# Sheaf scans in two places of the next block, two output buffers in the message phase, no gathers for empty tiles

## The chip, the cores and the metric

The kernel runs on one core of a Trainium2 chip. The metric is the device time of one execution in microseconds (us); three executions were timed. Engines are called PE (TensorE), DVE (VectorE), ACT (ScalarE), POOL (GpSimd) and SP (SyncE, which only issues DMAs here).

## The reference

The kernel computes four graph layers over 3,125 nodes with 64 features and 100,000 edges sorted by destination, each followed by a layer norm of the sum with its input:

```python
edge_index = jnp.stack([src, dst])
x = _layernorm(x + _L0_gnn_ref(x, edge_index, edge_attr_32, ...))   # edge MLP, mean and max by destination
x = _layernorm(x + _L1_gnn_ref(x, edge_index, ...))                 # four attention convolutions
x = _layernorm(x + _L2_gnn_ref(x, edge_index, ...))                 # sheaf layer
x = _layernorm(x + _L3_gnn_ref(x, ..., src, dst))                   # attention by node
```

The two that are touched here work per edge. In L0 each edge gets h = MLP([x[row], x[col], edge_attr]) with three matrices, and h is summed and maximised by destination. In L2 two small MLPs per edge give two 4x4 orthogonal matrices, made from Householder parameters, and msg = Fve^T Fue x[row] is summed by destination:

```python
Fve = _householder(_mlp(cat_ve, ...))
Fue = _householder(_mlp(cat_ue, ...))
msg = jnp.einsum('eka,ekb,ebh->eah', Fve, Fue, xjr) * (dis[col] * dis[row])[:, None, None]
agg = jax.ops.segment_sum(msg.reshape(-1, D * H), col, num_segments=n)
```

## The kernel before, in words

The edges are padded to 102,400, that is 800 tiles of 128 edges in four quarters of 200 tiles (T, QT). Only 782 tiles (T2) hold edges; the last 18 of quarter 3 are empty. A block takes tiles from all four quarters at once, so that the partitions of a block hold four stretches of the sorted edge list, and a segmented scan along the free dimension gives running sums (or maxima) by destination.

**Message phase** (`message_phase`, 50 blocks of 4 x 4 tiles, lines 355 to 690). For each block DVE writes the source indices (`stage`, L512), POOL issues 16 indirect DMAs that gather rows of a table into `got_s` (L486), PE transposes them into the PSUM bank p1 on top of the product of the edge features (L631, L636), and the block then goes through a chain: DVE adds the destination part (L553), ACT applies the bias and relu (L672), PE multiplies (L643), ACT (L674), PE (L647), ACT (L676), DVE runs two scans (L557, L559), PE transposes their results (L651), ACT copies them into `out_t` (L679) and issues four stores (L684). Behind the stores ACT waits until they have landed (L685), before it takes the next block's `gate` (L670) and relu (L672). In the first 44 blocks DVE also makes one-hot matrices in bf16, eight instructions a block (L518), PE multiplies them (`counts`, L614, four calls a block) and DVE adds the products to prefix counts (`evict`, L535): these count edges for a later phase. Blocks 44 to 49 do without. DVE's order is written out by hand: `stage` of block b + 1 stands at the head of the body of block b, so behind the scans of block b - 1. POOL's gather for a block waits for its `stage` and for L636 of the block two before.

**Sheaf phase** (`sheaf_phase`, 25 blocks of 8 x 4 tiles, lines 1419 to 1816). Block 0 is a block of self loops that needs no gather; blocks 1 to 25 are the edges. POOL issues 32 indirect DMAs a block (L1553) into one of three buffers. ACT copies a part of the gathered rows (`sources`, L1769), PE makes the hidden layer and the Householder entries (`hidden_and_entries`, L1704 to L1716) with an ACT relu between (`hide`, L1764), and ACT writes the entries out (`entries_out`, L1779 to L1783). DVE then makes the matrices (`messages`: L1604 to L1621), computes q, gprod, g and the four terms (L1625 to L1642), and PE turns the terms into the scan's layout in four pieces (`to_scan` 0 to 3, L1728, 32 matmuls each). Two PSUM banks hold the pieces, so `to_scan` 2 and 3 need scans 0 and 1 to be done. DVE scans the four pieces of block n - 1 (L1663) in one place of block n, between L1621 and L1625, behind `along` (L1589, the destination part of block n + 1). PE turns the sums back (`sums_back`, L1740), ACT copies them (L1798) and issues four stores (L1802). PE's order in body n: `turn_rows` (L1695), `sums_back` of n - 1 with `to_scan` 2 and 3 inside, `hidden_and_entries` of n + 1, wait for the messages of n, `to_scan` 0 and 1. ACT's order: `roots` (L1773), the sums of n - 1 and their stores, `sources`, `hide` and `entries_out` of n + 1. `stage` (L1582) of block n + 2 stands at the head of DVE's body n. POOL starts the first gather when the phase's memsets are done (`ready`). SP loads the next block's rows and masks when the four scans are done (L1528).

The two lines around which the message phase's part of the change turns, and the loop of the sheaf scans:

```python
                        act.dma_start(quarter[q, b], out_t[:, :, q, :]).then_inc(out_st, 16)
                    act.wait_ge(out_st, b * 64 + 64)
```
```python
                for j, (k, h) in enumerate(PIECES):
                    dve.wait_ge(turned, n * 4 + j - 3)
                    dve.tensor_tensor_scan(run[k][h][:, :], cont2[k][r][:, 512 * h:512 * h + 512], pin[j % 2][:, :],
```

Of the kernel before, what the change touches and what calls it, by code (L numbers as in the profile page):

```python
# [354 lines left out]
def message_phase(nc, io, dram, keep):  # L355
# [5 lines left out]
    with phase(nc, "ms") as ph:  # L361
# [26 lines left out]
        out_t = ph.sb("out_t", [P, ST, 4, 2 * M])  # L388
# [5 lines left out]
        scanned, turned, masked, turned_out, out_st = (ph.sem(n) for n in ("scanned", "turned", "masked", "turned_out", "out_st"))  # L394
# [14 lines left out]
        prefix = dram["prefix"][ND5:, :].rearrange("(i d) (h l) -> (d h) i l", d=ND5, l=LOW)  # L409

# [61 lines left out]
        def _(pool):  # L472
# [3 lines left out]

            def body(it):
                for u in range(2):
# [117 lines left out]
        def _(pe):  # L596
# [25 lines left out]
            def body(it, counting, last):  # L622
                for u in range(2):
# [10 lines left out]
                    for i in range(ST):  # L634
                        pe.wait_ge(got[u][i], it * 64 + 64)
# [24 lines left out]
        def _(act):  # L660
            act.wait_ge(weights, 16 * 24)

            act.sem_inc(turned_out, 1)

            def body(it):
                for u in range(2):
# [16 lines left out]
                    for q in range(4):  # L683
                        act.dma_start(quarter[q, b], out_t[:, :, q, :]).then_inc(out_st, 16)  # L684
                    act.wait_ge(out_st, b * 64 + 64)  # L685

            with act.Fori(0, NB // 2) as it:
                body(it)
            for u in range(2):
# [729 lines left out]
def sheaf_phase(nc, io, dram, keep):  # L1419
# [6 lines left out]
    with phase(nc, "sh") as ph:  # L1426
# [64 lines left out]

        def is_block(n, *blocks):
# [47 lines left out]
        def _(pool):  # L1540
# [3 lines left out]
            def body(c, it):  # L1544
                u, r = c % 2, c % RING
                pool.reg_add(turn, turn, 1)
# [13 lines left out]
        def _(dve):  # L1560
            dve.memset(w2[:, :], 0.0).then_inc(zero, 1)
            dve.memset(got_s[0][:, :, :], 0.0)
            dve.memset(zin[:, :, :], 0.0)
# [15 lines left out]
            dve.sem_inc(messaged, RING - 1)  # L1579

            def stage(b, u):
                dve.tensor_copy(st_src[u][:, :, :].rearrange("p i k -> p k i"),  # L1582
                                keep["src"][:, :].rearrange("p (k t) -> p k t", k=4)[:, :, ds(b * SB, SB)]).then_inc(staged, 1)
# [9 lines left out]
            def messages(n, r, s, between=lambda: None):  # L1593
# [542 lines left out]
```

## Time and profile before

| | |
|---|---|
| median of three runs | 4694.56 us (4692.95 to 4698.24) |
| the profiled execution's own time | 4687.18 us |
| its span | 4685.4 us |
| busy share of the span | PE 63%, PE weight loads 47%, DVE 65%, ACT 27%, POOL 40% |
| message phase | 209 to 1413 us |
| sheaf phase | 3087 to 4277 us |
| granted PE clock, mean | 0.66 of full in 325 to 1290 us, 0.80 in 3497 to 4130 us |

The span is the time from the first to the last instruction of one profiled execution. A busy share says how long an engine worked, not whether the rest waited for it. Rows of a timeline give start, duration, engine, line, operation, output and inputs; in square brackets stands how long the engine had been idle and what ended the wait. PEld is PE's weight load. SPq, ACTq and the like are an engine's sequencer, here issuing DMAs.

### The profile page before, as it was taken

The page shows a single profiled execution, that of the slowest core. Times are in us where ns is not written, and L with a number is a line of the kernel's source. Part 1 is how long each engine was busy: PE and PEld are TensorE (multiplying, and loading weights), DVE is VectorE, ACT ScalarE, POOL GpSimd, SP SyncE. Part 2 cuts the span into 40 slices and gives each one's busy share as a digit, 9 for nine tenths or more (in the row PEclk, how much of TensorE's full clock was granted, in tenths as well). Part 3 has the DMA queues.
Part 4 walks back from the last instruction along what each step waited for, and adds up shares of the span by engine and source line. Part 5 has one row for each costly group of instructions (what it writes and reads, how often), then busy time and mean ns, then how long its engine had stood idle before and what let it go on. Part 6 is the DMA issues. An engine that isn't in the chain of part 4 may idle for free. (4 is left out here: it accounts for less than half of the span.)

```text
span 4685.4 us, 59450 instructions
## 1 busy us (share of the span) xinstructions
PE 2968.8 (63%) x19382; PEld 2193.7 (47%) x19382; DVE 3034.2 (65%) x4651; ACT 1274.4 (27%) x1892; POOL 1881.9 (40%) x1835
## 2 busy tenths in 40 slices
PE   1055556566642477779799699515766667673676
PEld 1034444344421254546556466315665666663455
DVE  9466676667623488756556466446677767774796
ACT  0011111111110277535345245101111111110484
POOL 4577777677762121100000000067777677642000
PEclk9966666666665699989899899657878788876698
DMA  5156666555630488534234144044454554541342
GB/s 178 33 136 152 155 154 150 145 149 149 153 83 13 184 333 325 202 132 157 77 144 160 60 152 149 1 91 86 100 120 100 106 118 93 114 85 26 111 167 73
DMA packets 738112, 599.57 MB, mean 128 GB/s; under 512 B 486055, under 2 KB 676612, under 8 KB 714476
## 3 DMA queue, kind: packets, MB, share of 16 engines
q1 hardware_dynamic: 462650, 389.91, 28.4%
q0 software_dynamic: 64032, 141.68, 10.5%
q10 hardware_dynamic: 211282, 66.03, 6.0%
q8 instruction: 91, 1.49, 0.1%
q14 instruction: 57, 0.47, 0.0%
HBM read 396.80 MB, written 200.61 MB: 128 GB/s over the span
## 5 line engine op out<-in xcount | busy, mean ns | idle before, releaser
L486 POOL DMA_INDIRECT ms_got_s<-table_src,ms_st_src x800 | 845.7, 1057 | 339.8 <-issue 332.1
L1553 POOL DMA_INDIRECT sh_got_s<-sheaf_src,sh_st_src x800 | 783.9, 980 | 301.9 <-issue 239.2
L1728 PE MATMUL sh_pin<-ident,sh_term 128*128 128x128 f32 x3200 | 465.5, 317 | 129.0 <-DVE sh_run L1663 114.5
L1728 PEld LDWEIGHTS sh_pin<-ident,sh_term 128*128 128x128 f32 x3200 | 455.8, 232 | 135.1 <-DVE sh_run L1663 120.2
L1047 DVE CUSTOM_DVE_ANT_0 c_xs<-c_pa,c_logs 128x1024 f32<-128x1024 f32 (+1 forms) x400 | 379.0, 967 | 187.9 <-PE c_pa L1154 109.5
L126 POOL DMA_INDIRECT spread<-dst_tab,first_idx x25 | 24.3, 971 | 1133.1 <-DVEq L100 1125.8
L991 PE MATMUL c_pa<-c_esT,c_v 128*64 128x128 f32 (+1 forms) x5000 | 399.8, 286 | 86.2 <-DVE c_esT L1061 61.7
L991 PEld LDWEIGHTS c_pa<-c_esT,c_v 128*64 128x64 f32 (+1 forms) x5000 | 278.0, 138 | 224.7 <-issue 119.3
L973 PE MATMUL c_pa<-ident,c_xs 128*128 128x128 f32 x2500 | 370.3, 287 | 0.0
L1154 PE MATMUL c_pa<-c_kT,c_q_st 64*128 64x512 f32 (+1 forms) x800 | 340.7, 546 | 43.4 <-DVE c_peaks L1047 27.7
L614 PEld LDWEIGHTS ms_pc<-ms_hot_l,ms_hot_x 128*125 128x125 bf16 x1408 | 211.5, 208 | 283.6 <-issue 263.5
L614 PE MATMUL ms_pc<-ms_hot_l,ms_hot_x 128*125 128x256 bf16 (+1 forms) x1408 | 240.0, 342 | 148.5 <-DVE ms_hot_l L518 148.5
L1017 ACT ACTIVATE c_xs<-c_xs,c_neg 128x1536 f32<-128x1536 f32 x200 | 317.8, 1589 | 56.5 <-DVE c_neg L1056 56.1
L1157 PE MATMUL c_pa<-c_kT,c_q_st 64*128 64x512 f32 x600 | 323.0, 647 | 0.0
L535 DVE TENSOR_TENSOR ms_sums<-ms_pc,ms_sums 125x256 f32<-125x256 f32 x704 | 297.3, 422 | 27.7 <-DVE ms_run_max L559 9.6
L973 PEld LDWEIGHTS c_pa<-ident,c_xs 128*128 128x128 f32 x2500 | 276.9, 143 | 70.9 <-issue 70.6
L1011 ACT ACTIVATE c_esT<-c_pa 128x512 f32<-128x512 f32 (+1 forms) x400 | 203.8, 514 | 368.9 <-PE c_pa L973 368.3
L1061 DVE COPY c_esT<-c_pa 128x512 f32<-128x512 f32 x300 | 206.6, 689 | 137.0 <-PE c_pa L973 136.6
L1663 DVE TENSOR_TENSOR_SCAN sh_run<-sh_cont,sh_run,sh_pin 128x512 f32<-128x512 f32 x100 | 127.9, 1279 | 193.6 <-PE sh_pin L1728 188.4
L1642 DVE TENSOR_TENSOR sh_term<-sh_got_s,sh_pin 128x2048 f32<-128x2048 f32 x104 | 230.8, 2280 | 0.9
L1708 PE MATMUL sh_pz<-ident,sh_zin 128*128 128x128 f32 x416 | 93.7, 416 | 211.9 <-ACT sh_zin L1769 156.9
L1154 PEld LDWEIGHTS c_pa<-c_kT,c_q_st 64*128 64x128 f32 x800 | 137.9, 192 | 182.8 <-issue 132.5
(368 smaller groups left out, 5193.4 us busy)
## 6 DMA issues: line engine op xcount, KB each, us to landing
c_logs<-logs SPq DMA_DIRECT2D x75, 1562.5 KB, 6.5
prefix<-ms_sums SPq DMA_DIRECT2D x44, 1792.0 KB
logs<-c_logs SPq DMA_DIRECT2D x25, 1562.5 KB, 8.0
at_logs<-logs SPq DMA_DIRECT2D x25, 1562.5 KB
runs<-ms_out_t ACTq DMA_DIRECT2D x200, 128.0 KB
sh_cont<-cont SPq DMA_DIRECT2D x100, 256.0 KB
sums<-sh_out_t ACTq DMA_DIRECT2D x100, 256.0 KB
ms_seq<-in_dst_seq SPq DMA_DIRECT2D x200, 64.1 KB
```

The costliest lines, as they stand in the source:

```text
L486: pool.indirect_dma_start(got_s[u][:, i, q, :], None, dram["table_src"], bass.IndirectOffsetOnAxis(st_src[u][:, i, q:q + 1].bitcast(U32), ...
L535: dve.tensor_tensor(sums[u][:, at:at + 2, :], pc[j % 4][0:ND5 * HI, 2 * g:2 * g + 2, :], base.to_broadcast([ND5 * HI, 2, LOW]), ALU.add).t ...
L614: ins = pe.matmul(pc[j % 4][0:ND5 * HI, i:end, :], hot_x[k % 2][:, 4 * h + i, 0:ND5 * HI], hot_l[k % 2][:, 4 * h + i, :].rearrange("p (o n ...
L973: ins = pe.transpose(self.pa[0:m, 4 + g % 3, P * j:P * j + P], self.xs[i % self.ring][:, P * k:P * k + m], ident)
L991: ins = pe.matmul(self.pa[lo:lo + F, 7, 0:P], self.v[0:m, k, :], self.esT[0:m, k, :], start=(k < 2), stop=(k >= NC - 2), tile_position=(0, ...
L1017: act.activation(part, part, ACT.Exp, bias=self.neg[i % self.unroll][:, 0:1], accum_out=self.parts[:, ds(c * 2 + h, 1)]).then_inc(self.exp ...
L1047: dve.tensor_tensor_reduce(xs[:, lo:lo + m], scores(b, lo, m), logs[:, lo:lo + m], 1.0, -3e38, ALU.add, ALU.max, self.peaks[:, b:b + 1]).t ...
L1154: ins = pe.matmul(pa[:, 2 * (b % 2), 0:min(m, SW)], q[0:F, :], kT[0:F, lo:lo + min(m, SW)], start=True, stop=True, tile_position=(0, 0))
L1157: ins = pe.matmul(pa[:, 2 * (b % 2) + 1, 0:m - SW], q[F:P, :], kT[F:P, lo + SW:lo + m], start=True, stop=True, tile_position=(F, 0))
L1553: pool.indirect_dma_start(got_s[r][:, 4 * i + k, :], None, dram["sheaf_src"], bass.IndirectOffsetOnAxis(st_src[u][:, i, k:k + 1].bitcast(U ...
L1642: s.mark(dve.tensor_tensor(terms[k][:, :, :].rearrange("p t (a h) -> p t a h", a=4), got_s[r][:, :, 2 * H16 + H16 * b:2 * H16 + H16 * (b + ...
L1728: ins = pe.matmul(pin[j % 2][:, P * (i % 4):P * (i % 4) + P], term[:, 4 * i + 2 * k:4 * i + 2 * k + 2, :].rearrange("p t f -> p (t f)"), k ...
```

## The change

Message phase: `out_t` and the semaphore of its stores become pairs, and ACT waits for the store of two blocks before, just ahead of writing the buffer, instead of for its own store behind it. Both phases: the indirect DMAs of the 18 empty tiles are left out (blocks 45 to 49 and 23 to 25), and the counts that are waited for are lowered to match; POOL's loop in the message phase becomes 22 looped and 3 written-out pairs of blocks. Sheaf phase: the first two `stage` calls and the start of the gathers move ahead of the phase's memsets; the scans of pieces 0 and 1 move up to behind L1614, those of 2 and 3 stay behind `along`; PE does `to_scan` 2 and 3 together, then turns back pieces 0 and 1, makes the next block's entries, and only then turns back pieces 2 and 3; ACT takes `sources` of the next block ahead of the sums, and the stores to the end of its body.

```diff
-        out_t = ph.sb("out_t", [P, ST, 4, 2 * M])
+        out_t = [ph.sb(f"out_t{u}", [P, ST, 4, 2 * M]) for u in range(2)]
...
+        REAL = T2 - 3 * QT
+        def gathered(u, i, it):
+            if type(it) is not int:
+                return it * 64 + 64
+            return 16 * sum(4 - ((k * 2 + u) * ST + i >= REAL) for k in range(it + 1))
...
                         for q in range(4):
+                            if q == 3 and type(it) is int and (it * 2 + u) * ST + i >= REAL:
+                                continue
                             pool.indirect_dma_start(
...
-            with pool.Fori(0, NB // 2) as it:
+            with pool.Fori(0, WHOLE) as it:
+                body(it)
+            for it in range(WHOLE, NB // 2):
                 body(it)
...
-                        pe.wait_ge(got[u][i], it * 64 + 64)
+                        pe.wait_ge(got[u][i], gathered(u, i, it))
...
                     act.wait_ge(turned, b + 1)
+                    act.wait_ge(out_st[u], it * 64 + 64)
                     for of, lo in ((pts, 0), (p23, M)):
-                        ins = act.activation(out_t[:, :, :, lo:lo + M],
+                        ins = act.activation(out_t[u][:, :, :, lo:lo + M],
...
                     for q in range(4):
-                        act.dma_start(quarter[q, b], out_t[:, :, q, :]).then_inc(out_st, 16)
-                    act.wait_ge(out_st, b * 64 + 64)
+                        act.dma_start(quarter[q, b], out_t[u][:, :, q, :]).then_inc(out_st[u], 16)
...
-                pool.wait_ge(ready, 1)
+                pool.wait_ge(zero, 1)
                 pool.wait_ge(staged, now)
                 pool.wait_ge(messaged, now)
                 for i in range(SB):
                     for k in range(4):
+                        if k == 3 and is_block(n, *range(REAL // SB + 1, HB + 1)) and (n - 1) * SB + i >= REAL:
+                            continue
...
             dve.memset(w2[:, :], 0.0).then_inc(zero, 1)
-            dve.memset(got_s[0][:, :, :], 0.0)
-            dve.memset(zin[:, :, :], 0.0)
...
+            stage(0, 1)
+            stage(1, 0)
+            dve.sem_inc(messaged, RING - 1)
+            dve.memset(got_s[0][:, NC:TB, :], 0.0)
+            dve.memset(zin[:, NC:TB, :], 0.0)
...
                 s.do(dve.reciprocal(inverse[:, :, :, 0], dots[:, :, :, 0]))
+                middle()
...
-                for j, (k, h) in enumerate(PIECES):
+                for j in pieces:
+                    k, h = PIECES[j]
                     dve.wait_ge(turned, n * 4 + j - 3)
...
+                def middle():
+                    if not is_block(n, 1):
+                        scans(c - 1, it, (0, 1))
                 def between():
                     if not is_block(n, HB):
                         along(c + 1, it)
                     if not is_block(n, 1):
-                        scans(c - 1, it)
+                        scans(c - 1, it, (2, 3))
...
+            def rest_to_scan(n):
+                for j in (2, 3):
+                    pe.wait_ge(scanned, n * 4 + j - 5)
+                    to_scan(j)
+            def sums_back(n, pieces):
+                for j in pieces:
+                    k, h = PIECES[j]
                     pe.wait_ge(scanned, n * 4 + j - 3)
-                    if j + 2 < len(PIECES):
-                        to_scan(j + 2)
                     pe.wait_ge(copied, n * 4 + j - 3)
...
                 if not is_block(n, 1):
-                    sums_back(number(c - 1, it))
+                    rest_to_scan(last)
+                    sums_back(last, (0, 1))
                 if not is_block(n, HB):
                     hidden_and_entries(number(c + 1, it), (c + 1) % 2)
+                if not is_block(n, 1):
+                    sums_back(last, (2, 3))
                 pe.wait_ge(messaged, n + RING)
...
                 roots(n)
-                if not is_block(n, 1):
-                    sums_out(number(c - 1, it))
                 if not is_block(n, HB):
                     sources(c + 1, it)
+                if not is_block(n, 1):
+                    sums_out(last, (0, 1))
+                if not is_block(n, HB):
                     hide(number(c + 1, it))
                     entries_out(number(c + 1, it))
+                if not is_block(n, 1):
+                    sums_out(last, (2, 3))
+                    store(last)
```

## Rows read from the trace of the kernel before

**Rows 1.** Groups by line, 325 to 1290 us (busy us, mean ns; idle).
```profile
L486 POOL DMA_INDIRECT ms_got_s<-table_src,ms_st_src x641 | 687.6, 1073 | 281.1 <-issue 281.1
...
L518 DVE TENSOR_TENSOR ms_hot_l<-ms_iota,low 128x1024 bf16<-128x1024 bf16 x160 | 109.3, 683 | 0.0
...
L557 DVE TENSOR_TENSOR_SCAN ms_run_sum<-ms_cont,ms_run_sum,ms_h 128x512 f32<-128x512 f32 x40 | 51.4, 1286 | 163.6 <-ACT ms_h L676 163.6
```

**Rows 2.** Timeline of one counting block of the message phase, 930 to 956 us.
```profile
931.60 6.35 ACTq L684 DMA_DIRECT2D runs<-ms_out_t  x4
...
940.56 0.69 DVE L553 TENSOR_TENSOR ms_hin<-ms_p,ms_of_dst 128x512 f32<-128x512 f32 x1 [0.63 <-PE ms_p L636]
...
943.10 0.63 ACT L670 ACTIVATE ms_gate<-ms_cont 128x512 f32<-128x512 f32 x1 [11.65 <-DMA runs<-ms_out_t]
943.46 0.68 DVE L518 TENSOR_TENSOR ms_hot_l<-ms_iota,low 128x1024 bf16<-128x1024 bf16 x1
...
944.39 1.95 PE L643 MATMUL ms_p<-ms_h,ms_w 128*128 128x512 f32 x2 [2.84 <-ACT ms_h L672]
...
946.14 1.48 PE L614 MATMUL ms_pc<-ms_hot_l,ms_hot_x 128*125 128x256 bf16 x8
...
947.42 1.35 PE L647 MATMUL ms_p<-ms_h,ms_w 128*128 128x512 f32 x2
...
949.53 1.28 DVE L557 TENSOR_TENSOR_SCAN ms_run_sum<-ms_cont,ms_run_sum,ms_h 128x512 f32<-128x512 f32 x1 [3.68 <-ACT ms_h L676]
...
955.04 1.45 POOL L486 DMA_INDIRECT ms_got_s<-table_src,ms_st_src  x1 [2.23 <-issue]
```

**Rows 3.** Timeline of POOL: first gather of block 0, first of block 45.
```profile
216.37 1.00 POOL L486 DMA_INDIRECT ms_got_s<-table_src,ms_st_src  x1 [7.42 <-DVE ms_st_src L512]
...
1289.63 0.94 POOL L486 DMA_INDIRECT ms_got_s<-table_src,ms_st_src  x1 [2.02 <-issue]
```

**Rows 4.** Timeline of ACT, blocks 47 to 49 of the message phase.
```profile
1359.32 0.71 ACT L672 ACTIVATE ms_h<-ms_hin,ms_b 128x512 f32<-128x512 f32 x1
...
1371.53 2.18 ACTq L684 DMA_DIRECT2D runs<-ms_out_t  x4
...
1398.60 0.72 ACT L672 ACTIVATE ms_h<-ms_hin,ms_b 128x512 f32<-128x512 f32 x1 [2.37 <-DVE ms_hin L553]
```

**Rows 5.** Groups of POOL, 3140 to 3500, then 3550 to 4168 us.
```profile
L1553 POOL DMA_INDIRECT sh_got_s<-sheaf_src,sh_st_src x285 | 275.4, 966 | 86.9 <-issue 86.9
...
L1553 POOL DMA_INDIRECT sh_got_s<-sheaf_src,sh_st_src x449 | 441.5, 983 | 178.5 <-issue 132.8 <-DVE sh_st_src L1582 45.6
```

**Rows 6.** Timeline of one sheaf block, from 3854 to 3906 us.
```profile
3854.45 1.06 ACT L1769 ACTIVATE sh_zin<-sh_got_s 128x1024 f32<-128x1024 f32 x1 [6.21 <-issue]
...
3863.58 8.70 PE L1728 MATMUL sh_pin<-ident,sh_term 128*128 128x128 f32 x64
...
3865.02 0.32 DVE L1604 TENSOR_TENSOR sh_cross<-sh_low 128x128 f32<-128x128 f32 x1 [3.58 <-ACT sh_basis L1783]
...
3869.36 0.95 DVE L1614 RECIPROCAL sh_inverse<-sh_dots 128x128 f32<-128x128 f32 x1
...
3884.75 1.28 DVE L1663 TENSOR_TENSOR_SCAN sh_run<-sh_cont,sh_run,sh_pin 128x512 f32<-128x512 f32 x1 [4.83 <-PE sh_pin L1728]
...
3888.83 1.28 DVE L1663 TENSOR_TENSOR_SCAN sh_run<-sh_cont,sh_run,sh_pin 128x512 f32<-128x512 f32 x1 [2.80 <-PE sh_pin L1728]
...
3905.64 0.20 DVE L1582 COPY sh_st_src<-src 128x32 int32 x1 [0.28 <-DVE sh_term L1642]
```

**Rows 7.** Landing time of the sheaf gathers.
```profile
DMA to landing us min/median/max: 2.3/2.6/7.2
```

**Rows 8.** Timeline: start of the sheaf phase, and L1604 of its last block.
```profile
3087.36 0.10 DVE L1561 MEMSET sh_w<- 128x48 f32 x1 [39.72 <-PEq L104]
...
3099.83 1.01 POOL L1553 DMA_INDIRECT sh_got_s<-sheaf_src,sh_st_src  x1 [16.76 <-DVE sh_st_src L1582]
...
4216.28 0.33 DVE L1604 TENSOR_TENSOR sh_cross<-sh_low 128x128 f32<-128x128 f32 x1 [0.39 <-ACT sh_basis L1783]
```

More of the change, by code:

```diff
@@ L393, in message_phase @@
         multiplied, mm1, mm2, mm3, act1, act2, act3 = (ph.sem(n) for n in ("multiplied", "mm1", "mm2", "mm3", "act1", "act2", "act3"))
-        scanned, turned, masked, turned_out, out_st = (ph.sem(n) for n in ("scanned", "turned", "masked", "turned_out", "out_st"))
+        scanned, turned, masked, turned_out = (ph.sem(n) for n in ("scanned", "turned", "masked", "turned_out"))
+        out_st = [ph.sem(f"out_st{u}") for u in range(2)]
         dv, ds0, rows_turned, spread, added = (ph.sem(n) for n in ("dv", "ds0", "rows_turned", "spread", "added"))
@@ L663, in _ @@
             act.sem_inc(turned_out, 1)
+            for u in range(2):
+                act.sem_inc(out_st[u], 64)
             def body(it):
@@ L683, in body @@
                     for q in range(4):
-                        act.dma_start(quarter[q, b], out_t[:, :, q, :]).then_inc(out_st, 16)
-                    act.wait_ge(out_st, b * 64 + 64)
+                        act.dma_start(quarter[q, b], out_t[u][:, :, q, :]).then_inc(out_st[u], 16)
             with act.Fori(0, NB // 2) as it:
                 body(it)
+            for u in range(2):
+                act.wait_ge(out_st[u], 64 * (NB // 2) + 64)
             for u in range(2):
@@ L1490, in ring, with gathered @@
             return c % RING, it * (TURN // RING) + (c - 1) // RING
+        REAL = T2 - 3 * QT
+        def gathered(n):
+            if type(n) is not int:
+                return None
+            return 16 * sum(4 * SB - max(0, min(SB, m * SB - REAL)) for m in range(1, n + 1) if m % RING == n % RING)
         def is_block(n, *blocks):
@@ L1591, in along, with messages @@
                 dve.wait_ge(spread, n)
-            def messages(n, r, s, between=lambda: None):
+            def messages(n, r, s, middle=lambda: None, between=lambda: None):
                 dve.wait_ge(filled, n * 5 + 5)
@@ L1647, in messages @@
                 dve.sem_inc(messaged, 1)
-            stage(0, 1)
-            stage(1, 0)
             s = Steps(dve, dv)
@@ L1657, in _, with scans @@
             along(1, 0)
-            def scans(c, it):
+            def scans(c, it, pieces):
                 n, r = number(c, it), c % RING
-                for j, (k, h) in enumerate(PIECES):
+                for j in pieces:
+                    k, h = PIECES[j]
                     dve.wait_ge(turned, n * 4 + j - 3)
@@ L1676, in between @@
                     if not is_block(n, 1):
-                        scans(c - 1, it)
+                        scans(c - 1, it, (2, 3))
                 s = Steps(dve, dv, n * PER + LOOPS)
-                messages(n, r, s, between)
+                messages(n, r, s, middle, between)
                 assert s.n == PER
             loop(dve, body)
-            scans(TURN + 1, HB // TURN - 1)
+            scans(TURN + 1, HB // TURN - 1, (0, 1, 2, 3))
         @block.tensor
@@ L1743, in body @@
             def body(c, it):
-                n = number(c, it)
+                n, last = number(c, it), number(c - 1, it)
                 if not is_block(n, HB):
@@ L1791, in _, with sums_out @@
             entries_out(1)
-            def sums_out(n):
-                if not is_block(n, 1):
+            def sums_out(n, pieces):
+                if not is_block(n, 1) and 0 in pieces:
                     act.wait_ge(stored, n * 64 - 64)
-                for j, (k, h) in enumerate(PIECES):
+                for j in pieces:
+                    k, h = PIECES[j]
                     act.wait_ge(backed, n * 4 + j - 3)
@@ L1799, in sums_out, with store @@
                                    pout[:, :].rearrange("p (i k f) -> p i k f", i=4, k=2), ACT.Copy).then_inc(copied, 1)
+            def store(n):
                 act.wait_ge(copied, n * 4 + 1)
@@ L1804, in body @@
             def body(c, it):
[L1805 removed]
+                n, last = number(c, it), number(c - 1, it)
                 roots(n)
[L1807 to L1808 removed]
                 if not is_block(n, HB):
                     sources(c + 1, it)
+                if not is_block(n, 1):
+                    sums_out(last, (0, 1))
+                if not is_block(n, HB):
                     hide(number(c + 1, it))
                     entries_out(number(c + 1, it))
+                if not is_block(n, 1):
+                    sums_out(last, (2, 3))
+                    store(last)
             loop(act, body)
[L1815 removed]
+            sums_out(HB, (0, 1, 2, 3))
+            store(HB)
             act.wait_ge(stored, HB * 64)
```

21 lines of the change are left out of this document (9 added, 12 removed).

## The prediction

> **What bounds the kernel now.** I read the page first for the two phases in which POOL is the busiest engine, then groups by line in each, then timelines of single blocks. In the message phase the groups [rows 1] show a gather call of 1.073 us and 281.1 us of idle over 641 calls. The pause at a block start is 2.2 us (POOL at 955.04 in [rows 2]), 40 of them 88 us; the other (281.1 - 88) / 641 = 0.30 us lie between any two calls. A block of 16 calls thus occupies POOL for 16 x 1.374 = 22.0 us, but 641 calls, 40 blocks, took 965 us, 24.1 each. POOL has 2 us to spare. The loop that lasts 24.1 us is DVE's: `stage` of the next block stands behind the scans L557, and these waited 163.6 us in 40 blocks, 4.1 each, for ACT [rows 1]. The timeline [rows 2] shows why: ACT has issued its stores at 931.60 + 6.35 = 937.95, stands still until 943.10 for their landing, and takes the relu L672 at 943.6, though DVE had its input ready at 940.56 + 0.69 = 941.25.
>
> **Message phase, the wait for the store.** It goes; the wait for the store of two blocks before, one block time old or more, costs nothing. The relu then starts at 941.3 (gate and one DMA issue, 1.2 us behind 937.95, are over by 939.2). L643 runs from 942.05 for 1.95, to 944.0, and ACT's next step 0.7. PE's queue then holds `counts` 3, which needs the one-hots that end at 943.46 + 0.68 = 944.14, so no earlier than today's neighbours allow: 1.5 us, to 945.7. L647 1.35 to 947.0, ACT 0.7, scans at 947.75 in place of 949.53: 1.8 us. With the mean wait of 4.1 in place of this block's 3.68 it is 2.2. The DVE loop falls to 24.1 - 2.2 = 21.9, just under POOL's 22.0, and POOL becomes the bound: 22.05 a block. The first gather of block 45 starts at 216.37 + 45 x 22.05 = 1208.6 and not at 1289.63 [rows 3]: **81 us**. Lower bound: PE's order gives only 1.3 a block, 57 us. Upper: DVE's 21.9 from the start, 88 us.
>
> **Message phase, the end.** Blocks 45 to 49 lose 18 of 80 calls. At 0.98 + 0.30 the 62 left take 79.4 us, to 1288; landing, PE and DVE bring the last relu to 1292.5. ACT is next late: today's relu at 1359.32 leads to stores issued at 1371.53 + 2.18, a DMA issue 0.6 and the gate 0.6, so that the next relu could come at 1374.9, a loop of 15.6 [rows 4]; five of them from about 1214.5 also end at 1292.5. Today's is at 1398.60: the message phase gains **105 us**, 24 of them here (bounds 10, if ACT's loop stays near 19, and 26). The written-out bodies and the new semaphores cost nothing that any row shows.
>
> **Sheaf phase, what bounds it.** POOL's calls: 0.966 us and 86.9 / 285 = 0.305 between them, 40.7 a block in the first stretch; later 0.983, 41.0, but there POOL also waited 45.6 us for DVE's `stage` [rows 5]. So DVE's loop is longer: the body shown begins at 3865.02 - 3.58 - 0.20 = 3861.24 and the next at 3905.64, 44.4 us [rows 6]. Its lag uses up POOL's lead. It holds three waits: 3.58 for the entries, 4.83 and 2.80 for `to_scan` 2 and 3, which start only when the scans of 0 and 1 are done.
>
> **Sheaf phase, the new order.** I count from L1604 = 0. If the gathers are late, PE turns back the last two sums of the older block first (1.5, with ACT's entries between), and `to_scan` 0 and 1 take 8.7 to 10 [rows 6], to 11.5. DVE reaches the first scan place, behind L1614, at 5.3 (3869.36 + 0.95 - 3865.02), waits for both pieces, and leaves it at 12.8. `along` ended today before scans 0 and 1, at 3884.75 - 4.83 - 2.6 = 3877.3, 12.3 from L1604, so 7.0 of other work lie between: 19.8. PE meanwhile has turned the rows (about 1) and made pieces 2 and 3 (4.1 each, as 3888.83 - 3884.75) by 20.5. Scans end at 22.4, the rest of the block takes today's 3905.64 - (3888.83 + 1.28) = 15.5. That is 37.9 from L1604 to the end of the messages, with entries already there some 38.5 a block, and 36 where `to_scan` need not wait for them. ACT takes `sources` behind `roots` and no longer behind four stores; its store issue of 5 to 6 us moves to behind `entries_out`, where `roots` waits 13 us or more later. SP's loads follow the fourth scan as before, 20 us ahead of `turn_rows`. The new cost: ACT now waits for the next block's gather ahead of the sums, and PE's turning back of piece 1 and everything behind it hang on that. From landing to L1604 today 10.6 us pass (3854.45 to 3865.02); with the two sums and the of_dst matmul in front I take 14 (12 to 16). 14 + 37.9 = 51.9 is more than a block, but POOL has three buffers and its `stage` call comes 11 us after a landing where it is needed 41 after, so it is hidden. POOL therefore becomes the bound at 40.9 a block.
>
> **Sheaf phase, the sum.** The first gather waits today for the memsets, until 3099.83; in the new order for the first memset (3087.36), two stages and about 1 us: 3088.8 [rows 8]. Block 0's own chain hardly moves, and DVE catches up in two or three blocks. Gather 23 starts at 3088.8 + 22 x 40.9 = 3988.6 and lands (30 calls of 1.29, 2.6 to land [rows 7]) at 4029.9, L1604 of 23 is at 4043.9; from there DVE's 38.5 and 37 are longer than the shortened gathers: L1604 of block 25 at 4119.4, today 4216.28 [rows 8]. **97 us**, less 1 for what follows. Without the omitted calls it would be 3088.8 + 25 x 40.9 + 2.6 + 14 = 4127.9: they are worth 8. Bounds: 42.3 a block, if all 128 `to_scan` matmuls run at the slow pace and DVE stays the bound, gives 23 x 2.1 = 48 us; 40.0 a block gives 23 x 0.9 = 20 more than 96.
>
> **Sum.** 105 + 96 = 201 us. The profiled execution took 4687.2, so 4486; the median of the runs stands 7.4 higher, so 4494.
>
> **One rule against it.** POOL's calls take 1.073 in the counting blocks and 0.966 to 0.983 in the sheaf phase [rows 1, 5]; eight one-hot instructions of 0.68 us a block [rows 1] are what the first has more. The slowing is 16 x 0.10, under 2 us a block, and I carry it in the 22.0. The Trainium skill (SBUF — State Buffer, "Who interferes with whom") says that DVE and GpSimd share a port pair under an exclusive lock, held for the whole instruction, so that the other fully blocks. Taken so, POOL would lose 8 x 0.68 = 5.4 us on a block of 16 x 1.27 = 20.3 and need 25.7, more than the 24.1 measured, and the sum would be 4694.6 - 96 - 24 + 45 x 1.6 = 4647; the trace speaks against so full a block. Rival (b) is what is left of it.
>
> **The rivals.**
> (a) *The sheaf waits only move.* PE stays slow and DVE's loop is 42.3. For it: today piece 2 comes 4.83 + 1.28 = 6.1 us behind the scan that frees its bank, piece 3 only 4.1 behind that. Against: PE now stands still less. 4694.6 - 105 - 48 = 4542.
> (b) *The counting blocks gain nothing*, because POOL is held up by DVE's one-hots as soon as it no longer pauses, or because the relu's 2 us are lost again at `counts` 3. The pause of 2 us then only turns into longer calls. Gain 24 + 96 = 120: 4575. Against: the one-hots are as many as before, and slow a call by 0.10.
> (c) *Slower.* ACT's wait for the gather of n + 1 ahead of the sums of n - 1 puts gather, entries, messages in series: 51.9 a sheaf block in place of 44.4, 7.5 x 24 = 180 lost where 96 were gained; with the message phase's 105 that is 4770. It decides once a sheaf block costs more than 44.4 + 105 / 24 = 48.8. Against: three buffers, and a `stage` 30 us early.
> (d) *The change doesn't do what it says*: ACT's wait had cover, its 11.65 us being DMA issue rather than waiting, and the sheaf loop is held at 44.4 by something unseen: 4694.
>
> **How the numbers follow.** Forecast 0.78, with its own range 4460 to 4530; (a) 0.12, (b) 0.05, (c) 0.04, (d) 0.01. The likeliest gives 4494. The range 4458 to 4545 takes in (a) and the forecast's bounds and leaves out (b) to (d) and a tenth of the forecast. About 0.2%, 9 us, is what a measurement of this kernel can tell from no change. Faster 0.95, same 0.01, slower 0.04.
>
> **What would show it.** ACT's gate no longer waits for the DMA to `runs`; POOL's pauses at block starts in the message phase shrink from 2.2 to 0.3, its block takes 22, and it starts block 45 at about 1209. L557's wait falls to about 2. In the sheaf phase POOL starts at 3088.8 less the message gain and never waits for L1582; L1604 waits several us for the entries each block, the third and fourth L1663 hardly, the second 2 to 5. Both indirect DMA groups count 782. Wrong would be: a POOL block near 24 in the message phase, POOL waiting for L1582 in the sheaf phase, or more than 100 us of waits of ACT's L1769 that push L1604's period past 42.

## The result and the profile after

The kernel after took **4470.03 us** (median of 4, 4465.49 to 4474.15), the kernel before beside it 4695.58: ratio 0.9519 [0.9503, 0.9536], 226 us less; the forecast was 4494. A second comparison gave 4470.57 (5 runs), ratio 0.9525 [0.9507, 0.9544]. The profiled execution took 4467.3 us, its span 4465.5.

I cut the span where SyncE issues the first transfer of the next phase, since that is seen at the same place in every kernel. The message phase ends at 1287.07 (before 1415.99): 128.9 us gained, 105 forecast. Between it and the sheaf phase 1.7 more are gained. The sheaf phase lasts from 2956.64 to 4061.82, 1105.2 us, where it was 3087.26 to 4279.72, 1192.5: 87.3 gained, 96 forecast. Of the rest of the program 2 us are gained, in code that the change doesn't touch. Each phase length here is that of one profiled execution, and the same code differs between kernels and between executions: the sheaf phase of the kernel before takes 1192.5 there and 1198.8 in the first experiment below, that of the kernel after 1105.2, 1105.6 in its second comparison and 1103.3 in the run without the one-hots.

The groups of the message phase, 325 to 1190 us, beside [rows 1] (busy us, mean ns; idle and what ended it):
```profile
L499 POOL DMA_INDIRECT ms_got_s<-table_src,ms_st_src x643 | 669.5, 1041 | 196.0 <-issue 194.5 <-PE ms_p L651 1.5
...
L533 DVE TENSOR_TENSOR ms_hot_l<-ms_iota,low 128x1024 bf16<-128x1024 bf16 x159 | 108.7, 684 | 0.0
...
L572 DVE TENSOR_TENSOR_SCAN ms_run_sum<-ms_cont,ms_run_sum,ms_h 128x512 f32<-128x512 f32 x40 | 51.4, 1284 | 55.1 <-ACT ms_h L693 55.1
```
POOL's idle is 0.30 a call, no more: no pause is left at a block start. The calls themselves are shorter too, 1.041 for 1.073. The scan L572 waits 1.4 us a block for ACT, where it waited 4.1.

The timeline of one counting block, beside [rows 2] (start us, us, engine, line; idle before and what ended it):
```profile
922.42 5.57 ACTq L702 DMA_DIRECT2D runs<-ms_out_t  x4
928.56 0.99 ACTq L686 DMA_DIRECT2D cont<-ms_cont  x1
929.60 0.63 ACT L687 ACTIVATE ms_gate<-ms_cont 128x512 f32<-128x512 f32 x1 [7.42 <-issue]
932.86 0.72 ACT L689 ACTIVATE ms_h<-ms_hin,ms_b 128x512 f32<-128x512 f32 x1 [2.63 <-DVE ms_hin L568]
...
938.42 1.28 DVE L572 TENSOR_TENSOR_SCAN ms_run_sum<-ms_cont,ms_run_sum,ms_h 128x512 f32<-128x512 f32 x1 [0.98 <-ACT ms_h L693]
```
ACT's gate follows its own DMA issues and no landing, and the relu L689 now waits for DVE's input where DVE's input waited for the relu. The granted PE clock rose beside it, from 0.66 of full (325 to 1290 us before) to 0.74 (755 to 1190 us).

POOL's first gather of block 45, beside [rows 3], and the pair of first gathers of the sheaf phase, beside [rows 8]:
```profile
1184.54 0.94 POOL L499 DMA_INDIRECT ms_got_s<-table_src,ms_st_src  x1 [0.30 <-issue]
...
2957.72 1.01 POOL L1583 DMA_INDIRECT sh_got_s<-sheaf_src,sh_st_src  x1 [5.28 <-DVE sh_st_src L1594]
2959.03 0.95 POOL L1583 DMA_INDIRECT sh_got_s<-sheaf_src,sh_st_src  x1 [0.30 <-issue]
```
Block 45 starts 105.1 us earlier than before, so 23.8 of the 128.9 belong to the end of the phase.

The groups of POOL in the sheaf phase, 2957 to 3045, then 3400 to 3900 us, beside [rows 5]:
```profile
L1583 POOL DMA_INDIRECT sh_got_s<-sheaf_src,sh_st_src x65 | 68.1, 1047 | 24.8 <-issue 19.5 <-DVE sh_st_src L1594 5.3
...
L1583 POOL DMA_INDIRECT sh_got_s<-sheaf_src,sh_st_src x389 | 382.6, 984 | 118.6 <-issue 118.6
```
POOL never waits for `stage` again. A block costs it 43.3 us twice at the start and 32 x (0.984 + 0.305) = 41.2 later.

One sheaf block, beside [rows 6], with its L1637 (the old L1604), its scans L1696 (the old L1663) and PE's L1765 (the old L1728):
```profile
3501.78 1.06 ACT L1814 ACTIVATE sh_zin<-sh_got_s 128x1024 f32<-128x1024 f32 x1 [9.37 <-DMA sh_got_s<-sheaf_src,sh_st_src]
...
3515.47 0.33 DVE L1637 TENSOR_TENSOR sh_cross<-sh_low 128x128 f32<-128x128 f32 x1 [2.32 <-ACT sh_basis L1828]
...
3516.89 8.25 PE L1765 MATMUL sh_pin<-ident,sh_term 128*128 128x128 f32 x64
...
3521.61 1.28 DVE L1696 TENSOR_TENSOR_SCAN sh_run<-sh_cont,sh_run,sh_pin 128x512 f32<-128x512 f32 x1 [0.85 <-PE sh_pin L1765]
...
3525.19 1.28 DVE L1696 TENSOR_TENSOR_SCAN sh_run<-sh_cont,sh_run,sh_pin 128x512 f32<-128x512 f32 x1 [2.29 <-PE sh_pin L1765]
3525.86 7.31 PE L1765 MATMUL sh_pin<-ident,sh_term 128*128 128x128 f32 x64
...
3533.38 2.60 DVE L1696 TENSOR_TENSOR_SCAN sh_run<-sh_cont,sh_run,sh_pin 128x512 f32<-128x512 f32 x2
```
The first two scans wait 3.1 us together, the last two not at all (before 7.6). From ACT's L1814 to L1637 13.7 us pass (14 forecast). ACT waits for the gather in front of L1814. DVE's L1637 waits 2.3 us for the entries behind it, which is no loss while POOL is the bound.

### The profile page after: what moved, and what is told of

Same layout as the page of the kernel before. It is cut to its first block and busy times, and to the rows that moved or that the text cites. A ratio compares the mean times of both kernels' runs of the same rounds, so it can differ in the third digit from the quotient of the medians.

```text
span 4465.5 us, 59437 instructions
## 1 busy us (share of the span) xinstructions
PE 2862.2 (64%) x19382; PEld 2081.9 (47%) x19382; DVE 3035.0 (68%) x4651; ACT 1271.7 (28%) x1892; POOL 1837.4 (41%) x1799
## 5 line engine op out<-in xcount | busy, mean ns | idle before, releaser
L499 POOL DMA_INDIRECT ms_got_s<-table_src,ms_st_src x782 | 810.6, 1037 | 245.5 <-issue 235.9
L1765 PE MATMUL sh_pin<-ident,sh_term 128*128 128x128 f32 x3200 | 413.9, 297 | 23.0 <-DVEq L1681 23.0
L1765 PEld LDWEIGHTS sh_pin<-ident,sh_term 128*128 128x128 f32 x3200 | 411.5, 214 | 24.5 <-DVEq L1681 24.5
L1173 PE MATMUL c_pa<-c_kT,c_q_st 64*128 64x512 f32 (+1 forms) x800 | 340.5, 547 | 43.2 <-DVE c_peaks L1066 27.6
L629 PE MATMUL ms_pc<-ms_hot_l,ms_hot_x 128*125 128x256 bf16 (+1 forms) x1408 | 209.3, 310 | 194.2 <-DVE ms_hot_l L533 193.7
L629 PEld LDWEIGHTS ms_pc<-ms_hot_l,ms_hot_x 128*125 128x125 bf16 x1408 | 173.3, 180 | 323.8 <-issue 323.8
L1781 PE MATMUL sh_pout<-ident,sh_run 128*128 128x128 f32 x400 | 86.9, 358 | 237.5 <-ACT sh_out_t L1844 237.5
L1696 DVE TENSOR_TENSOR_SCAN sh_run<-sh_cont,sh_run,sh_pin 128x512 f32<-128x512 f32 x100 | 128.0, 1280 | 104.0 <-PE sh_pin L1765 100.1
```

Source lines behind the costliest of these rows:

```text
L499: pool.indirect_dma_start(got_s[u][:, i, q, :], None, dram["table_src"], bass.IndirectOffsetOnAxis(st_src[u][:, i, q:q + 1].bitcast(U32), ...
L629: ins = pe.matmul(pc[j % 4][0:ND5 * HI, i:end, :], hot_x[k % 2][:, 4 * h + i, 0:ND5 * HI], hot_l[k % 2][:, 4 * h + i, :].rearrange("p (o n ...
L1173: ins = pe.matmul(pa[:, 2 * (b % 2), 0:min(m, SW)], q[0:F, :], kT[0:F, lo:lo + min(m, SW)], start=True, stop=True, tile_position=(0, 0))
L1765: ins = pe.matmul(pin[j % 2][:, P * (i % 4):P * (i % 4) + P], term[:, 4 * i + 2 * k:4 * i + 2 * k + 2, :].rearrange("p t f -> p (t f)"), k ...
```

## The experiments

**The two output buffers alone**, in the kernel before:
```diff
-        out_t = ph.sb("out_t", [P, ST, 4, 2 * M])
+        out_t = [ph.sb(f"out_t{u}", [P, ST, 4, 2 * M]) for u in range(2)]
...
+                    act.wait_ge(out_st[u], it * 64 + 64)
...
-                    act.wait_ge(out_st, b * 64 + 64)
```


> The kernel before with the pair of output buffers in the message phase alone. My theory (POOL becomes the bound of the counting blocks, and its block start no longer falls on the one-hots): POOL never pauses at a block start, its block takes 21.5 us, the first gather of block 45 starts at 1184 and the end of the phase is bound by POOL's 16 calls at 20.3 us a block. The message phase ends 105 to 110 us earlier, total 4588 (4583 to 4595). Rival, that the shorter loop came from a faster PE clock or from fewer gathers and not from the store wait: under 60 us, 4635 or more.

4590.88 us, ratio 0.9793 [0.9776, 0.981]. The phase ends at 1309.32, 106.7 earlier. POOL in 325 to 1190 us, and its first gather of block 45:
```profile
L487 POOL DMA_INDIRECT ms_got_s<-table_src,ms_st_src x643 | 670.1, 1042 | 196.0 <-issue 195.1 <-PE ms_p L637 0.9
...
1185.01 0.94 POOL L487 DMA_INDIRECT ms_got_s<-table_src,ms_st_src  x1 [0.30 <-issue]
```
The counting blocks are those of the kernel after to 0.5 us in 968: everything there comes from the buffers. The granted PE clock rises with this edit alone too, to 0.74 (755 to 1190 us); what the clock would give by itself no run separates. Its sheaf phase lasts 1198.8 (before 1192.5); nothing in it was changed.

**The omitted gathers alone**, in the kernel before:
```diff
+                            if q == 3 and type(it) is int and (it * 2 + u) * ST + i >= REAL:
+                                continue
...
+                        if k == 3 and is_block(n, *range(REAL // SB + 1, HB + 1)) and (n - 1) * SB + i >= REAL:
+                            continue
```


> The kernel before without the 18 empty gathers in both phases, nothing else. My theory: in the message phase ACT's loop of 19.4 us (store wait included) holds the last five blocks, so that only about 5 us of the 23 come out; in the sheaf phase DVE's loop is the bound and nothing comes out. Total 4690 (4684 to 4695). Rival, that a gather left out is worth its 1.28 us everywhere: 2 x 23 us, 4650.

4684.66 us, ratio 0.9992 [0.998, 1.0003]: no difference that can be told. The message phase ends at 1409.05, 7 earlier, the sheaf phase lasts 1200.7, no shorter. ACT in two of its late message blocks:
```profile
1338.26 0.70 ACT L684 ACTIVATE ms_h<-ms_hin,ms_b 128x512 f32<-128x512 f32 x1
...
1356.06 0.63 ACT L682 ACTIVATE ms_gate<-ms_cont 128x512 f32<-128x512 f32 x1 [5.76 <-DMA runs<-ms_out_t]
1356.60 0.71 ACT L684 ACTIVATE ms_h<-ms_hin,ms_b 128x512 f32<-128x512 f32 x1
```
Its loop is 18.3 us: still the landing of the runs. With both, the kernel after's late blocks cost POOL 18.3 once and then 15.4 to 15.8, and its message phase ends 22 us ahead of that with the buffers alone. Fewer calls are worth 22 with the second buffer and at most 7 without: two kernels whose message phase is the same code, the kernel before and the next one, also end it 7 apart (1415.99 and 1423.26).

**The sheaf order alone**: the scans' two places with the new order of PE and ACT, in the kernel before; no early start, no omitted gathers.
```diff
-                    if not is_block(n, 1):
-                        scans(c - 1, it)
+                    if not is_block(n, 1):
+                        scans(c - 1, it, (2, 3))
...
+                    rest_to_scan(last)
+                    sums_back(last, (0, 1))
```


> The kernel before with the new order of the sheaf phase alone: scans in two places, PE's and ACT's new order; no early start, no omitted gathers, one output buffer in the message phase. My theory: POOL is the bound of the sheaf phase from block 1 on at 41.5 us a block, L1604's last start lies 3099.83 + 25 x 41.5 + 2.6 + 14 = 4154 against 4216: 62 us, total 4633 (4625 to 4645). The message phase's gather calls stay at 1.07 us in the mean, with a slow first call (1.35) in each block. Rival, that DVE's loop is only shortened to 42.5 or so and still the bound: 45 us, and POOL waits for the stage call.

4614.19 us, ratio 0.9839 [0.9823, 0.9856]. The sheaf phase lasts 1127.7, 65 less (62 expected), with POOL at 41.3 a block and never pausing: the theory's mechanism. The total lies 11 below the expected range. The profiled execution took 4640.08, 26 above the median, and spent 7 us more in the message phase and 9 more between the phases than that of the kernel before, in code that is the same, so the total says less than the phase.

**The kernel after without the early start**: POOL waits for `ready` again, the two stages stand behind the memsets.
```diff
-                pool.wait_ge(zero, 1)
+                pool.wait_ge(ready, 1)
```


> The kernel after, with the first stage calls, POOL's first gather and the full memsets of the sheaf phase back in their old place. My theory (POOL is the bound of that phase all the way): 11 us later, POOL's first call 12 us behind the phase's start and never a pause behind it; total 4481 (4477 to 4485). Rival, that the chain of block 0 on DVE hides POOL's start, as it does in the first blocks: under 3 us, 4472.

4482.51 us, ratio 0.955 [0.9534, 0.9565]. The total fits the theory, but by accident. Between the two profiled executions lie 16.1 us: 10.7 have arisen by the start of the sheaf phase and 2.9 arise behind it, where the edit can't reach, and 2.4 in the phase. So small effects must be read from the phase. POOL's first gather:
```profile
2980.10 1.00 POOL L1583 DMA_INDIRECT sh_got_s<-sheaf_src,sh_st_src  x1 [16.91 <-DVE sh_st_src L1613]
```
This is 12.7 us into the phase, in the kernel after 1.1; the last gather comes 4.7 later, the phase lasts 1107.6 for 1105.2. The 11.6 us are there as forecast, but they shrink: blocks 1 and 2 of the kernel after take 43.2 and 43.4 us, here 43.9 and 41.5, the next twenty 41.3 on average, here 41.1, and the end of the phase hides half of what is left. The sheaf phase of the kernel after takes 1103.3 to 1105.6 in three profiles, so that the early start is worth 2 to 4 us, near what the rival gave it. Why its blocks take 0.2 longer stays open.

**ACT's order**: the sums of pieces 0 and 1 ahead of the next block's `sources`, in the kernel after.
```diff
-                if not is_block(n, HB):
-                    sources(c + 1, it)
                 if not is_block(n, 1):
                     sums_out(last, (0, 1))
+                if not is_block(n, HB):
+                    sources(c + 1, it)
```


> The kernel after, with ACT taking the sums of pieces 0 and 1 ahead of the next block's sources, so that PE's turning back no longer hangs on the gather. My theory (POOL sets the pace, and the time from a gather's landing to the entries shows only behind the last gather): the way from landing to L1637 shortens by 3 to 4 us from 13.7, the blocks stay at 41.3 us, and the phase ends 0 to 4 us earlier: 4468 (4463 to 4472). Rival, that the wait for the gather in front of the sums does cost in each block: 20 us or more gained, 4450.

4475.42 us, ratio 0.9528 [0.9512, 0.9544], which can't be told from the kernel after; the sheaf phase lasts 1107.3. From `sources` to L1637 12.7 us pass on average, for 15.2 in the kernel after, so the way is 2.5 shorter, and the phase doesn't end earlier for it. The 20 us of the rival aren't there: rival (c)'s place, ACT's wait ahead of the sums, costs nothing that shows.

**All four scans in one place**, with all else of the kernel after:
```diff
-                    if not is_block(n, 1):
-                        scans(c - 1, it, (0, 1))
+                    pass
...
-                        scans(c - 1, it, (2, 3))
+                        scans(c - 1, it, (0, 1, 2, 3))
```


> The kernel after, but with all four scans again in one place, behind along; PE's and ACT's new order stays. If the split is what shortens DVE's loop: the loop is 12.3 to the scans, 2.6 for the first two, to_scan 2 and 3 of 6 and 4, and 15.5, 41 to 43 us from L1637 to the end of the messages, just over POOL's 41.3; POOL pauses for the stage call in the later blocks, and the kernel loses 5 to 30 us, 4485. Rival, that the new order of ACT and PE alone was enough (the wait for the entries of 4 us gone from a loop of 44.4): loop 40.5, no pause, within 4 us of the kernel after.

4483.5 us, ratio 0.955 [0.953, 0.9569]; the sheaf phase 1114.0, 9 longer. What VectorE waited for from 3050 to 3900 us (total us, times, longest), in this kernel:
```profile
DVE sh_run L1696 <- PE sh_pin L1764: 134.6, 40, 5.4
DVE sh_of_dst L1622 <- PE sh_pd L1731: 23.2, 18, 2.3
DVE sh_cross L1637 <- ACT sh_basis L1827: 7.0, 2, 6.1
```
and in the kernel after:
```profile
DVE sh_cross L1637 <- ACT sh_basis L1828: 91.6, 17, 13.0
DVE sh_run L1696 <- PE sh_pin L1765: 75.8, 40, 2.3
```
With one place DVE hardly waits for the entries: its own loop is 40.9 in most blocks and 41.1 on average, as long as POOL's 41.0. POOL never pauses, and starts block 23 even 7.6 us earlier in the phase than in the kernel after, as its calls are shorter here (0.973 for 0.984 in 3400 to 3900 us). The loss comes in the last blocks, where calls are left out and POOL gets faster. L1637 of them with one place:
```profile
3969.75 0.32 DVE L1637 TENSOR_TENSOR sh_cross<-sh_low 128x128 f32<-128x128 f32 x1 [0.23 <-DVE sh_term L1676]
...
4010.44 0.33 DVE L1637 TENSOR_TENSOR sh_cross<-sh_low 128x128 f32<-128x128 f32 x1 [0.23 <-DVE sh_term L1676]
```
and in the kernel after:
```profile
3962.89 0.33 DVE L1637 TENSOR_TENSOR sh_cross<-sh_low 128x128 f32<-128x128 f32 x1 [0.23 <-DVE sh_term L1676]
...
3997.97 0.33 DVE L1637 TENSOR_TENSOR sh_cross<-sh_low 128x128 f32<-128x128 f32 x1 [0.23 <-DVE sh_term L1676]
```
40.7 and 35.1 us apart, neither waiting for anything; over the last three such distances one place costs 10.6 us. So the expected 5 to 30 us are lost, but not by pauses of POOL: the rival had the loop right (40.5, no pause) and missed the end of the phase.

**The counting blocks without VectorE's one-hots**, in the kernel after. The matrices stay zero and with them the counts; PE's products and DVE's additions remain.
```diff
+                dve.sem_inc(generated, 1)
-                for hot, of, n in ((hot_x, "cell", XW), (hot_l, "low", LOW)):
-                    ins = dve.tensor_tensor(
...
-                ins.then_inc(generated, 1)
```


> The kernel after without DVE's one-hot instructions in the message phase (they are left out, the matrices stay zero, so the counts of edges are wrong and with them the second layer). If it is these that slow POOL's calls: the mean call there falls from 1.040 to 0.96 or 0.98 as in the last blocks, POOL's block from 21.5 to 20.3, and the first gather of block 45 starts at 216.4 + 45 x 20.3 = 1130 instead of 1185. Rival, that the calls are slowed by the DMA load or by other DVE work (scans, evictions with an SBUF and a PSUM input): the mean stays over 1.02.

4466.9 us (one run). The calls shrank as expected, to 0.973 on average, but the blocks hardly did: 21.25 us, block 45 at 1175.07 and not at 1130, with POOL pausing again at 28 block starts. POOL from 325 to 1190 us, then ACT in one block:
```profile
L499 POOL DMA_INDIRECT ms_got_s<-table_src,ms_st_src x650 | 632.7, 973 | 233.0 <-issue 231.2 <-PE ms_p L648 1.8
```
```profile
897.70 6.41 ACTq L699 DMA_DIRECT2D runs<-ms_out_t  x4
904.28 2.32 ACTq L683 DMA_DIRECT2D cont<-ms_cont  x1
906.65 0.63 ACT L684 ACTIVATE ms_gate<-ms_cont 128x512 f32<-128x512 f32 x1 [9.11 <-issue]
907.19 0.70 ACT L686 ACTIVATE ms_h<-ms_hin,ms_b 128x512 f32<-128x512 f32 x1
```
The relu L686 waits for nothing but ACT's own five DMA issues, 9.1 us long. DVE's scans wait 5.3 us a block for ACT, where they wait 1.4 in the kernel after. So ACT's loop, with POOL no longer ahead of it, is 20.2 to 22.2 us a block.

**One gather in four left out**, in the kernel after, in all blocks of both phases; those parts of the buffers hold zeros.
```diff
-                            if q == 3 and type(it) is int and (it * 2 + u) * ST + i >= REAL:
+                            if q == 3:
                                 continue
...
-                        if k == 3 and is_block(n, *range(REAL // SB + 1, HB + 1)) and (n - 1) * SB + i >= REAL:
+                        if k == 3:
                             continue
```


> The kernel after, with one gather in four left out in both phases (the q = 3 of each tile in the message phase, the k = 3 in the sheaf phase; those buffer parts hold zeros, so the messages of these edges are not the reference's). 12 calls per message block take 12 x 1.34 = 16.1 us and 24 per sheaf block take 24 x 1.28 = 31 us, so GpSimd no longer sets the pace and what comes next shows. Message phase, theory: not VectorE (16.9 us of work a block with the one-hots) but ScalarE's ring: copies of the runs, five transfers issued, gate, three activations with TensorE between them, scans, transposes, as in the run without one-hots, whose blocks stayed at 20.2 to 22 us while GpSimd paused: blocks of 20 to 22 us again. Rival: VectorE or nothing else in particular, blocks of 17 to 18 us, the message phase 170 us shorter. Sheaf phase: the last two blocks of the kernel after had L1637 37.4 and 35.1 us apart with no wait for a gather, so 35 to 38 us a block here, 85 to 150 us less for the phase. Whole kernel, theory 4320 to 4380 us, rival 4150 to 4200 us.

4325.9 us (one run). POOL's blocks stay at 20.5 and 20.6 us in most of the message phase, with pauses at the block starts, though 12 calls need 16.7. The number is the theory's, the cause is not. ACT's relu waits for `hin`, 1.6 us a block on average, and POOL for `stage`:
```profile
900.88 1.45 POOL L499 DMA_INDIRECT ms_got_s<-table_src,ms_st_src  x1 [3.46 <-issue]
...
907.37 0.63 ACT L689 ACTIVATE ms_gate<-ms_cont 128x512 f32<-128x512 f32 x1 [7.25 <-issue]
910.64 0.72 ACT L691 ACTIVATE ms_h<-ms_hin,ms_b 128x512 f32<-128x512 f32 x1 [2.64 <-DVE ms_hin L570]
```
DVE's own row of instructions, 16.4 us of work a block with 3.7 of short waits in it, most of them for PE and ACT, makes the loop. DVE's loop, 20.55 in most blocks here, and ACT's, 21.2 on average in the run without the one-hots, are thus both within 5% of POOL's 21.5. The sheaf phase lasts 982.9, its blocks 36.0 on average.

**The same with all scans in one place:**
```diff
-                        scans(c - 1, it, (2, 3))
+                        scans(c - 1, it, (0, 1, 2, 3))
```


> The thinned kernel (one gather in four left out in both phases, so the messages of these edges are not the reference's) with all four scans of a block in one place, as in the run with one place. Theory: the two places shorten VectorE's loop itself, from 40.7 us (the distance of L1637 in the last blocks of the one-place run, where it waited for nothing) to 35 to 38, and the kernel after hides most of that behind GpSimd's 41 us: here sheaf blocks of 40 to 41 us, the phase about as long as in the kernel after and 85 to 130 us longer than in the thinned kernel with two places. Rival: VectorE's loop in the steady blocks is the same for both, and the 12 us between one place and two come from the tail alone: the two thinned kernels within 15 us of each other.

4437.53 us (one run), the sheaf phase 1107.3, its blocks 41.1. DVE's scans from 3100 to 3800 us, here, then with two places:
```profile
L1701 DVE TENSOR_TENSOR_SCAN sh_run<-sh_cont,sh_run,sh_pin 128x512 f32<-128x512 f32 x68 | 87.0, 1279 | 123.5 <-PE sh_pin L1769 119.4
```
```profile
L1701 DVE TENSOR_TENSOR_SCAN sh_run<-sh_cont,sh_run,sh_pin 128x512 f32<-128x512 f32 x78 | 99.8, 1280 | 54.2 <-PE sh_pin L1770 50.0 <-DVE sh_inverse L1652 0.2
```
7.3 us of waits a block (17 blocks) against 2.8 (19.5), which is 4.5 of the 5 us by which the two places shorten DVE's loop. Over the phase that is 124 us, once POOL is out of the way, as the theory had it. In the change itself they are worth 9.

## Why the prediction was right, and where not

**The path.** The forecast was 4494 with a range of 4458 to 4545, and 4470.03 was measured. The path is right in both phases: POOL became the bound, without a pause. Between the two profiled executions, 4687.2 and 4467.3, the gain is 220 for 201: the message phase gave 24 more, the sheaf phase 9 less, and 4 come from between and behind them.

**Message phase, the wait for the store.** The mechanism stands: ACT's wait for the landing is gone, its relu no longer holds DVE. The term of 81 was mis-sized; it is 105. It went by 22.05 a block, and POOL took (1184.54 - 216.41) / 45 = 21.51. The step that failed is "POOL's block is 16 x 1.374": I took the mean call of the trace before as fixed, the pause aside. But in it the first call of each block followed `stage` by a moment, and so fell on DVE's next one-hots, as POOL's row in [rows 2] with its 1.45 shows. In blocks 5 to 43 it took 1.353 on average and the other fifteen 1.054; in the kernel after, where POOL runs ahead of `stage`, 0.944 and 1.048. (1.353 - 0.944) + 15 x 0.006 = 0.50 of the 0.54. The pause cost 2.0 beyond the usual 0.30 and another 0.4 in the call behind it. With the buffers alone the first call takes 1.035 and the others 1.043: which calls are long differs between the two kernels, the mean of all (1.041 and 1.042) and the gain do not.

**DVE's 21.9.** I had DVE's loop just under POOL's. By the thinned kernel it is 20.55, so my estimate was 1.35 long, and POOL's margin was 1 us where I had 0.1. With so thin a margin it was partly luck that POOL came out as the bound.

**Message phase, the end.** 23.8 for 24. ACT's loop came down to 15.7, where I gave 15.6 (gates at 1206.82, 1222.98, 1237.91, 1254.03), with 3.05 to 3.57 us of issues in it. The lower bound, a loop near 19, is what the omitted gathers alone show (18.3).

**Sheaf phase, the block.** Forecast 40.9, measured 43.3 twice, then 41.3: block 23 starts 13 us later than forecast against the phase. The step is the call time: I went near the 0.966 of the first stretch in [rows 5], and it was 1.047 in the first two blocks, 0.984 later, which is the second stretch's 0.983. Why it is 0.984 and not 0.966 stays open: in 3400 to 3900 us it is 0.973 with one place, 0.977 without the early start and 0.991 with ACT's sums first, and no run separates what DVE does at the moment of a call.

**Sheaf phase, DVE.** I gave 38.5 and 37 for the last blocks; they took 37.4 and 35.1, so that of the 13 us 4 came back and L1637 of the last block stands 1041.3 us into the phase, for 1032.0 forecast. The thinned kernel shows 36.0 in the middle, the value I gave for the case in which `to_scan` waits for no entries. Two more terms were off. The omitted calls were to be worth 8; from the sheaf order alone to the kernel without early start they are worth 1127.7 - 1107.6 = 20, nearly their 18 x 1.29 = 23, as DVE had the reserve to follow; 2 of the 20 have arisen by block 23, ahead of the first omitted call, by shorter calls. The early start was to shift everything by 11 and is worth 2 to 4. That the two together are nearly right, 19 forecast and some 22 measured, is luck.

**The two places themselves.** The working bundled them with PE's and ACT's order and never asked how they share. One place with the new order, the early start and the omitted gathers gives 1114.0 for 1192.5, nearly everything; a DVE loop of 41.1 for 44.4 is already enough to meet POOL's. The wait for the entries, some 4 us a block before, is gone there. Whether PE's or ACT's order removes it, no run separates: ACT's sums were put first only where POOL hides DVE's loop.

**The rivals.** (a) fell: DVE's loop is 36, not 42.3. (b) fell: 105 us in the counting blocks, and shorter calls. What is left of it shows only without the one-hots: they cost POOL 16 x (1.041 - 0.973) = 1.1 us a block. The Trainium skill (SBUF — State Buffer, "Who interferes with whom") lets a VectorE instruction with two SBUF inputs, as the one-hots are, contend only with a GpSimd instruction that reads SBUF, and says that a probe saw no stall of DMAs by `tensor_tensor`. A full block by eight one-hots of 0.68 would be 5.4 us, by estimate; this case shows a fifth of that, so neither a full block nor none. (c) fell: ACT stood 215 us in front of L1814 in 20 blocks, and L1637 kept POOL's period on average (41.1 from block 4 to 23, single blocks 37.4 to 47.9); having the sums first gained nothing. (d) fell: the gate waits for no landing, and the 44.4 are gone.

**The parts don't add.** Alone they give 99 (buffers), 76 (sheaf order) and 5 (omitted gathers, not told from none): 180. Together with the early start they give 226. In the missing 46 lie 15 us of omitted gathers in the message phase (22 for 7), 20 in the sheaf phase (20 for none) and 2 to 4 of the early start; the other 7 to 9 are within what two kernels differ by in code that is the same in both.

## What to carry to other kernels

When a wait is removed and another engine takes over as the bound, that engine's instruction time must be taken from the moments in which it wasn't restarting: its first instruction after a pause may fall on work that it would else be clear of. Savings on an engine that isn't the bound (fewer gathers here: 5 us alone, some 42 in the set) have to be costed in the state that the other edits leave behind, and a shortened loop behind the bound is worth what its margin lets through: 9 us here for 124 in reserve. Small parts are read from their own phase, since the stretch between the two phases, which no edit touches, took from 1669.0 to 1682.3 us in these kernels; and even an untouched sheaf phase differed by 6.

## What the runs showed of the hardware

Five DMA issues hold ScalarE, in the kernel after, for 6.9 to 9.2 us in the counting blocks 5 to 43 and for 3.05 to 3.57 in the last five blocks: the same five transfers, nothing waited for but the issue. SyncE beside the issues of 922.42 us shown above, and the issues of a late block:
```profile
922.10 6.40 SPq L470 DMA_DIRECT2D prefix<-ms_sums  x2
...
1203.81 2.20 ACTq L702 DMA_DIRECT2D runs<-ms_out_t  x4
1206.19 0.59 ACTq L686 DMA_DIRECT2D cont<-ms_cont  x1
```
The kernel after by stretches (length, then busy us and count of PE, PEld, DVE, ACT and POOL; granted clock, DMA share, GB/s):
```profile
755.00:1190.00 435.00, 253.21 (x1159) 168.90 (x1159) 330.07 (x597) 76.03 (x120) 336.84 (x323) 0.74 0.68 169
...
1190.00:1280.00 90.00, 51.77 (x138) 27.91 (x139) 27.51 (x31) 21.23 (x34) 57.70 (x58) 0.59 0.37 78
```
The DMA engines' share fell from 0.68 to 0.37 with it. Another thing goes at the same time: in each of the 44 counting blocks SyncE issues its two stores of the counts (`prefix`) 0.3 to 1.5 us ahead of ScalarE's four, and in the last blocks it issues none. Which of the two lengthens ScalarE's issues was not tried; the one-hots don't, for without them they take 7.5 to 9.4 us. Where VectorE and GpSimd leave it room, in the run without the one-hots, ScalarE's loop is 20 to 22 us by these issues. It is busy only 76.03 / 20.2 = 3.8 us a block in the kernel after, so a table of busy shares doesn't show it.

A gather call of GpSimd takes 0.94 us at its shortest and in the median, with 0.30 between two. In blocks 5 to 43 of the kernel after 26% of the calls take over 1.0 us, most of those 1.1 to 1.4; without the one-hots it is 6%. The first call behind a pause took 1.35 on average in the kernel before, and 1.35 in the thinned kernel, where POOL pauses again; without the one-hots and with 25 pauses in blocks 1 to 43 it took 0.97. So it is the one-hots under it, not the pause, that lengthen it.
